# Sign counts on ScalarE, thirty of fifty rows on VectorE: a graph network kernel's first chunks

## What is computed

```python
h = relu(layernorm(x))
deg = segment_sum(ones, src)                   # edges of each node
feat = h * clip(deg, 1)**-0.5
x = x + relu(segment_sum(feat[src], dst)) @ W.T + b
h = relu(layernorm(x))
msg = h[src] @ W_msg.T + b_msg + edge_embed[edge_type]
x = x + gru_cell(segment_sum(msg, dst), h)     # gates r, z, n
```

## Time and profile before

| | us |
|---|---|
| median of 3 runs | 938.37 (937.33 to 938.54) |
| the profiled execution | 936.48 |
| its span in the profile | 934.5 |
| TensorE busy (share of the span) | 848.2 (91%) |
| VectorE busy | 776.1 (83%) |
| ScalarE busy | 503.8 (54%) |

### The profile page before, as it was taken

How to read it: one execution, slowest core, us unless ns; L and a number is a source line. 1 busy time by engine, 2 the same in 40 slices (tenths; PEclk the granted TensorE clock), 3 DMA queues, 4 the chain that set the end, 5 groups by cost and what they waited for, 6 DMA issues and landing times.

```text
span 934.5 us, 21030 instructions
## 1 busy us (share of the span) xinstructions
PE 848.2 (91%) x8962; PEld 757.1 (81%) x8962; DVE 776.1 (83%) x1043; ACT 503.8 (54%) x924; POOL 86.5 (9%) x77
## 2 busy tenths in 40 slices
PE   2264999999999999999999999799999999999996
PEld 2252888888888888888888888688898889888985
DVE  6897999999999999999999982386667667766876
ACT  1479588888888888888888873111111110111111
POOL 6880203010020010100000000000000000000000
PEclk9999999999999999999999999899999999999999
DMA  4541434356443365433355300766776676667650
GB/s 111 113 163 46 163 144 174 145 208 231 155 170 149 144 234 208 160 145 149 144 208 207 154 7 13 200 237 223 280 279 233 242 287 257 236 251 294 244 220 21
DMA packets 38595, 169.41 MB, mean 181 GB/s; under 512 B 8140, under 2 KB 21651, under 8 KB 35552
## 3 DMA queue, kind: packets, MB, share of 16 engines
q1 hardware_dynamic: 32188, 160.25, 45.7%
q0 software_dynamic: 6000, 6.48, 2.6%
q10 hardware_dynamic: 308, 1.28, 0.5%
HBM read 87.93 MB, written 80.00 MB: 180 GB/s over the span
## 4 chain that ended last, share of the span: by engine, by line
PE 74%; ACT 12%; POOL 4%; DVE 4%; issue 3%; DMA 2%; SPq 0%; ACTq 0%; DVEq 0%; POOLq 0%
PE ps L1285 27%; PE ps L1156 23%; PE ps L1145 12%; ACT ring L952 7%; POOL tab L483 3%; PE ps L1249 2%; PE ps L1250 2%; PE ps L1168 2%; PE ps L1182 2%; DMA tab<-dst 1%; ACT tab L963 1%; PE ps L1255 1%; PE ps L1254 1%; DVE work L725 1%; DMA tab<-dst,row_i 1%
## 5 line engine op out<-in xcount | busy, mean ns | idle before, releaser
L1145 PE MATMUL ps<-work 128*128 128x106 f16 x3125 | 429.0, 216 | 48.7 <-ACT ring L952 29.7
L1156 PE MATMUL ps<-ring,tab 125*128 125x250 f16 x2500 | 413.2, 272 | 0.7 <-ACT ring L957 0.7
L952 ACT ACTIVATE ring<-ps 128x848 f16<-128x848 f32 x375 | 329.8, 882 | 73.9 <-PE ps L1145 68.6
L1145 PEld LDWEIGHTS ps<-work 128*128 128x128 f16 x3125 | 288.5, 101 | 68.3 <-ACT ring L952 28.2
L1285 PE MATMUL ps<-ring,tab 125*128 125x250 f16 (+1 forms) x2500 | 276.8, 269 | 0.0
L1285 PEld LDWEIGHTS ps<-ring,tab 125*128 125x128 f16 (+1 forms) x2500 | 242.5, 97 | 28.6
L1156 PEld LDWEIGHTS ps<-ring,tab 125*128 125x128 f16 x2500 | 244.4, 98 | 25.1 <-ACT ring L957 0.9
L725 DVE TENSOR_TENSOR work<-iota_row,mch 128x3906 f16<-128x3906 f16 x100 | 222.0, 2220 | 5.6 <-PE ps L1145 4.5
L732 DVE TENSOR_TENSOR work<-iota_w,mch 128x1550 f16<-128x1550 f16 x200 | 188.3, 983 | 0.0
L813 DVE TENSOR_TENSOR work<-work,ring 125x3250 f16<-125x3250 f16 (+1 forms) x92 | 161.6, 1779 | 0.0
L1094 ACT ACTIVATE tab<-ps,bg 128x250 f32<-128x250 f32 x25 | 11.7, 470 | 155.4 <-PE ps L1250 155.4
(11 more groups left out here) (167 smaller groups left out, 595.1 us busy)
## 6 DMA issues: line engine op xcount, KB each, us to landing
adjacency<-ring SPq DMA_DIRECT2D x23, 2937.5 KB
ring<-adjacency SPq DMA_DIRECT2D x46, 812.5 KB, 6.4
ring<-adjacency SPq DMA_DIRECT2D x46, 750.0 KB, 9.2
adjacency<-ring SPq DMA_DIRECT2D x23, 183.1 KB
h_turned<-hst SPq DMA_DIRECT2D x25, 125.0 KB, 2.0
tab<-h_turned SPq DMA_DIRECT2D x25, 125.0 KB, 2.0
out<-x_sb SPq DMA_DIRECT2D x25, 125.0 KB
x_sb<-x SPq DMA_DIRECT2D x3, 560.0 KB
```

Of the source, the lines that this page charges most:

```text
L952: act.activation(to(x * 2 * u, 2, x), ps[:, s:s + 2, 0:x * SLOTS].rearrange("p b (x h) -> p h b x", h=SLOTS), ACT.Copy).then_inc(sem("evac ...
L1145: last = pe.matmul(ps[:, 2 * (u % 2) + i // BANKW, o:o + WCOLS], lohot[:, s, k, :], combo[:, s, k, :], start=True, stop=True)
L1156: mm = pe.matmul(psD[c % 2], tabv[0][P, h, s, :], adj[c % 2][P, h, :], start=i == 0, stop=i == 2 * BLOCKS - 1)
```

## The change

1. ScalarE counts the first nodes too, for steps 3 and 4: `search_odd` becomes `search_signs`, which is called with "odd" as before and with "even" for these steps, over 66 values with a new limit `thr_even`, right behind the odd counts. VectorE's `search_runs` for steps 3 and 4 go; in their place one `take_runs` behind chunk 1's first batch makes `run0` and `run_i` of both steps out of the sums.
2. `ON_ACT` is 2 instead of 3: VectorE makes batches 2, 3 and 4 of the rows, 30 of 50.
3. ScalarE's row keys for chunks 3 to 5 come after unit 6 of chunk 1 instead of after unit 10.
4. In chunk 0 VectorE takes the statistics of x's fourth fifth before it unpacks chunks 1 and 2, instead of after.
5. The factor: `a0 = (var + eps)` is made with the statistics, max and product are one instruction, and 4096 goes into the square root's scale.

```diff
-ON_ACT = 3
+ON_ACT = 2
...
+SIGNED = [("odd", g) for g in range(STEPS[3][1])] + [("even", g) for g in range(*STEPS[3])] + \
+         [("odd", g) for g in range(*STEPS[4])] + [("even", g) for g in range(*STEPS[4])] + \
+         [("odd", g) for g in range(*STEPS[5])]
...
+            gp.iota(thr_even[:, :], [[2 * WIN, CHUNKS]], base=-1, channel_multiplier=2 * BLOCKS,
+                    allow_small_or_imprecise_dtypes=True)
...
+        def take_runs(v, ch, first, last):
+            at = slice(STEPS[first][0], STEPS[last][1])
+            signed = SIGNED.index(("even", STEPS[last][1] - 1)) + 1
+            for k in range(JUNK):
+                v.wait_ge(sem(f"signs{k}"), len(range(k, signed, JUNK)))
+            ch.did(v.scalar_tensor_tensor(run0[P, at], even_sum[P, at], 0.5, row[P, at], ALU.mult, ALU.add))
+            ch.wait()
+            ch.did(v.tensor_scalar(run0[P, at], run0[P, at], HLEN / 2, None, ALU.add))
+            ch.wait()
+            v.tensor_scalar(run_i[P, at], run0[P, at], 3.0, None, ALU.mult).then_inc(sem("run_i"), last + 1 - first)
...
+            v.scalar_tensor_tensor(a0[P, :], deg[P, :], 1.0, a0[P, :], ALU.max, ALU.mult).then_inc(sem("a_square"), 1)
             ch.did(v.tensor_reduce(flags[P, 3:4], odd_sum[P, :], AX, ALU.max))
-            ch.wait()
-            ch.did(v.tensor_scalar(degm[P, :], deg[P, :], 1.0, None, ALU.max))
-            ch.did(v.tensor_scalar(a0[P, :], xvar[P, :], 1.0 / D, EPS, ALU.mult, ALU.add))
-            ch.wait()
-            v.tensor_tensor(a0[P, :], a0[P, :], degm[P, :], ALU.mult).then_inc(sem("a_square"), 1)
...
-            ch.wait()
-            ch.did(v.tensor_scalar(a0[P, :], a0[P, :], HSCALE, None, ALU.mult))
...
                         if b == 1:
+                            row_stats(v, ch, 3, 0, XB)
                             unpack(v, ch, 1, 2)
-                            row_stats(v, ch, 3, 0, XB)
-                            search_runs(v, ch, 3)
...
-                        if b == 3:
-                            search_runs(v, ch, 4)
                     if c == 1:
+                        if b == 0:
+                            take_runs(v, ch, 3, 4)
...
-        def search_odd(act, m):
+        def search_signs(act, which, m):
...
+            limit, n, to = {"odd": (thr_odd, CAND, odd_sum), "even": (thr_even, HLEN, even_sum)}[which]
...
-                    if c == 1 and u == ROOT_UNIT + ON_ACT_UNITS:
-                        high_rows(act, 3)
+                    if c == 1 and u == ROOT_UNIT + 2:
                         row_keys(act, AHEAD, AHEAD)
...
-                        search_odd(act, ODD_AT[u])
+                        search_signs(act, "odd", ODD_AT[u])
+                        if ODD_AT[u] < 5:
+                            search_signs(act, "even", ODD_AT[u])
```

More of the change, by code:

```diff
@@ L71 @@
 runs_in0 runs_in1 runs_in2 runs_in3 runs_in4 runs_in5
-squares sq_sum wm_norm gsc_set scaled g_col emb_in odd0 odd1 a_square a_root scale0 h0 rows_v tab0_hi tab0
+squares sq_sum wm_norm gsc_set scaled g_col emb_in signs0 signs1 a_square a_root scale0 h0 rows_v tab0_hi tab0
 fields lo_keys turned mch_keys mch onehot built spent evac adj_out0 adj_out1 types_moved
@@ L187, in gnn @@
         thr_odd = sb("thr_odd", [128, CHUNKS], F32)
+        thr_even = sb("thr_even", [128, CHUNKS], F32)
         thr_key = sb("thr_key", [128, CHUNKS], F32)
@@ L205, in gnn @@
         deg = sb("deg", [128, BLOCKS], F32)
-        degm = sb("degm", [128, BLOCKS], F32)
         outdeg = sb("outdeg", [128, BLOCKS], F32)
@@ L261, in gnn @@
         totals, at = carve(early, at, CHUNKS)
+        even_sum, at = carve(early, at, CHUNKS)
         tri, at = carve(early, at, 128)
@@ L645, in join_stats @@
             ch.wait()
+            ch.did(v.tensor_scalar(a0[P, :], xvar[P, :], 1.0 / D, EPS, ALU.mult, ALU.add))
+            ch.wait()
         def scale_weights(v, ch):
@@ L676, in scale_rows @@
             for k in range(JUNK):
-                v.wait_ge(sem(f"odd{k}"), len(range(k, CHUNKS, JUNK)))
+                v.wait_ge(sem(f"signs{k}"), len(range(k, len(SIGNED), JUNK)))
             ch.did(v.scalar_tensor_tensor(run1[P, :], odd_sum[P, :], 0.5, row[P, :], ALU.mult, ALU.add))
@@ L789, in vector_build @@
                         if b == 2:
-                            rows_vector(v, ch, 3)
-                            rows_vector(v, ch, 4)
+                            for t in range(ON_ACT, TBATCHES):
+                                rows_vector(v, ch, t)
                         if b >= 2:
@@ L897, in vector_layer1 @@
             post1_out_vector(v, last)
-        def search_odd(act, m):
+        def search_signs(act, which, m):
             a, b = STEPS[m]
+            limit, n, to = {"odd": (thr_odd, CAND, odd_sum), "even": (thr_even, HLEN, even_sum)}[which]
             act.wait_ge(sem(f"cand_in{m}"), 16 * (b - a))
             for g in range(a, b):
-                positive(act, sem(f"odd{g % JUNK}"), g // JUNK)
-                act.activation(signs[P, g % JUNK, :], cand[P, g, :], ACT.Sign, bias=thr_odd[P, g:g + 1], scale=-2.0,
-                               accum_out=odd_sum[P, g:g + 1]).then_inc(sem(f"odd{g % JUNK}"), 1)
+                made, k = divmod(SIGNED.index((which, g)), JUNK)
+                positive(act, sem(f"signs{k}"), made)
+                act.activation(signs[P, k, 0:n], cand[P, g, 0:n], ACT.Sign, bias=limit[P, g:g + 1], scale=-2.0,
+                               accum_out=to[P, g:g + 1]).then_inc(sem(f"signs{k}"), 1)
         def row_keys(act, g, n):
@@ L1032, in scalar_main @@
             act.activation(gsc[:, :], psB, ACT.Sqrt, bias=least[:, :]).then_inc(sem("wm_norm"), 1)
-            search_odd(act, 0)
-            search_odd(act, 1)
+            search_signs(act, "odd", 0)
+            search_signs(act, "odd", 1)
             row_keys(act, 0, 1)
             turn_scalar(act, 0)
-            search_odd(act, 2)
+            search_signs(act, "odd", 2)
             for c in range(CHUNKS):
@@ L1045, in scalar_main @@
                         act.wait_ge(sem("a_square"), 1)
-                        act.activation(a0[P, :], a0[P, :], ACT.Sqrt).then_inc(sem("a_root"), 1)
+                        act.activation(a0[P, :], a0[P, :], ACT.Sqrt, scale=1.0 / HSCALE ** 2).then_inc(sem("a_root"), 1)
                         act.wait_ge(sem("scale0"), 1)
```

5 lines of the change are left out of this document (3 added, 2 removed).

## The result

The changed kernel takes **940.53 us** (median of 6 executions, 939.43 to 941.93), the kernel before 938.12 in the same comparison (936.38 to 938.87). The ratio is 1.0031 with a 95% interval of 1.0019 to 1.0042, so +2.9 us (+1.8 to +3.9). That is outside what I called "within 0.2%" (1.9 us), and the median lies 0.4 us above my range. Its profiled execution took 939.75 us with a span of 937.8. Of before that was 936.48 and 934.5 us.

A forecast was written before the change was run, and what follows sets the result against it. The chain to TensorE's bank at 119.42 us was taken as the bound: GpSimd's gathers, ScalarE, then VectorE. +3.26 − 0.22 + 2.58 − 4.93 = +0.69 us at VectorE's pnm gave 939.1 us, range 935.9 to 940.1.

The forecast's parts named there:

- within 0.2%: Whole kernel's time: a difference of up to 1.9 us either way, which measurement cannot tell from no change; chance 0.76.
- my range: Measured time of the changed kernel: 935.9 to 940.1 us, including 0.6 us for the spread of the runs.
- The rule of held issues: GpSimd's gather issues: one that begins inside a VectorE one-hot is held and ends 1.08 us after that instruction.
- GpSimd's extra iota costs between nothing and 0.17 … I take nothing: GpSimd ahead of the first gather: the added iota was counted as free, covered by VectorE's and TensorE's own work.
- The landing lag of 2.19 us: Last candidate gather: from the end of its issue on GpSimd to ready data takes 2.19 us, as before.
- The even counts: ScalarE's counts for steps 3 and 4: 0.34 us each, between 0.28 and 0.40, with VectorE waiting 3 us.
- The short factor, the rows and the row keys: VectorE up to pnm: −0.22 us for one operation less, +2.58 for ten more rows, −4.93 for the removed wait.
- TensorE has room: TensorE up to 119.42 us: 80 products start at 96.1, its bank comes 0.86 us before release, not setting the end.
- the slot: Rival: GpSimd's issue at 39.31 gets in ahead of the one-hot; −1.2 us, 937.2 us, chance 0.25.
- GpSimd is not delayed: Rival: the candidate gather issues come no later than before; −2.3 us, 936.1 us, chance 0.16.
- slow products: Rival: TensorE's 80 products of chunk 0 stay at the low clock level; +6 us, 944.5 us, chance 0.05.
- Carrying the profile's difference to the median: Whole kernel: the profiled execution's 1.89 us below the median was added, turning a span of 935.2 into 939.1 us.

The follow-up runs named there:

- run 4: Changed kernel with two statistics of x's fourth fifth made twice, right ahead of chunk 0's one-hots of batch 2: 938.32 us against 937.43 before.
- run 5: Changed kernel with the statistics of x's fourth fifth moved back behind the unpacking of chunks 1 and 2: 939.66 us against 937.59 before.
- run 2: Changed kernel with the iota of thr_even moved late, behind the one of thr_key: 939.22 us against 937.59 before.
- run 1: Kernel before with one more iota of 25 elements on GpSimd behind the one of thr_odd: 938.50 us against 937.59 before.
- run 3: Changed kernel with SyncE's write of chunk 0's adjacency held until step 5's gathers are in: 939.21 us against 937.43 before.
- run 7: Changed kernel with 20 rows on VectorE again and the row keys back at their old place: 943.05 us against 938.39 before.
- run 6: Kernel before with 30 rows on VectorE and ScalarE's row keys four units sooner: 935.29 us against 937.59 before.
- run 12: Kernel before with 30 rows on VectorE, row keys sooner, TensorE's constants wait behind 25 matmuls and the short factor: 934.12 us against 938.39 before.
- run 8: Kernel before with only the row keys of chunks 3 to 5 four units sooner: 937.55 us against 938.39 before.

## Why the prediction was wrong, step by step

- **The rule of held issues** (in the part on GpSimd's issues): right, and shown by run 4. In the fourteen profiles, between 24 and 66 us, 167 issues began inside a one-hot, and 166 ended 1.06 to 1.10 us after it. Its two held issues of the changed order took 3.2 and 3.1 us as replayed, each at the predicted time + 0.8 to 0.9. Incomplete: run 5's issue is the one left, and lost four times in a row.
- **"GpSimd's extra iota costs between nothing and 0.17 … I take nothing"**: this step failed. It cost 0.91 in the changed kernel's start; undoing it gave back 0.8 (run 2), and alone it cost 0.86 there and +0.8 in the median (run 1). The cover I named (VectorE's and TensorE's own work) was not there: TensorE's first matmuls wait for GpSimd's last constant, and between the iota and that stood two operations that run into VectorE's instruction. Of the kernels with the early iota (the changed one, runs 1, 3, 4, 5, 7) all six profiles show 0.8 and 1.0 us; of the eight others two do (runs 6 and 12). So 0.9 is the difference of these two profiles; against a median of executions that collide now and then the price is somewhat less. I had written down the rule for gather issues and did not ask where else it applies.
- **The landing lag of 2.19 us**: carried over from an order in which SyncE's write was issued 0.91 us after the gather's issue had ended. The gather's end moved by 4.35 us and the write by 3.33, so they met. Mis-sized by 0.71; shown by run 3 and by the lags by distance.
- **The even counts** (0.34 at pitch): the trace has 0.33. `take_runs` waits 2.93, I said 3. The last one-hot starts at 60.19; predicted 59.1 and 0.91 for the start are 60.0. This is the 0.2 that is left.
- **The short factor, the rows and the row keys**: −2.57 predicted, −2.54 measured. Rows and keys alone are −2.35 by the terms and −2.3 in the kernel before (run 6). But they are no two separate terms: the keys alone give −0.9 and not −4.9 (run 8).
- **TensorE has room**: right in what it says of the end, not of the way there. The 80 products start at 98.83 and not at 96.1, and take 8.75 us instead of 9.63. Its bank is at 121.93, where it waits 1.48 us for ScalarE, which waited 1.55 for `pnm`.
- **The rivals**: the slot was not won (the one-hot at 40.07 is ahead of 40.12), though 0.05 us decided; with 0.4 us of extra work it is won. "GpSimd is not delayed" and "slow products" did not come: over 96 to 106 us the granted clock was 1.00 in the changed kernel and 0.91 in the one before.
- **Carrying the profile's difference to the median**: I took 1.89 us. The changed kernel's profiled execution is only 0.78 under its median. Before's had the shortest exchange between the layers of all (last section), and it lacked the collision at the start, as six of the eight without the early iota do. How much of its 1.89 either makes is not measured. From `pnm`'s +2.52 and before's median the time would have been 940.6.
- **The range** ended 0.4 us too low. It held ±0.36 for one small count and 0.6 for the spread of the runs, and nothing for the two terms that I had carried over as constants.

## What to carry to other kernels

In this kernel gather issues that began inside a two-input VectorE instruction were held, and `ident` and `nident` took longer there (0.78 and 1.04 us for 0.52 and 0.53). Not everything was: the iota and the memset behind them take 0.13 and 0.20 us inside that instruction in both kernels, and issues that began inside VectorE's statistics (one input) took 1.21, as at 45.42. So an added or moved instruction is to be priced at the next such meeting behind it, not at its own length: 0.1 us made the first gather 0.9 late, and 0.4 us of extra work won 2. A DMA's landing time is no constant: when a chain moves, look at which large transfers do not move by the same amount. An edit that removes a wait is worth what the next wait leaves of it, on the same engine or on another, so find that one and pay for both together (−0.9 alone, −2.3 as a pair).

## What the runs showed of the hardware that I had not expected

**A held issue can miss the gap.** In 166 cases of 167 it ended 1.06 to 1.10 us after the end of the one-hot in which it had begun; in run 5 one ended only after the fourth, and what was different there is open.

**The time from `pnm` to the end varies by itself.** In thirteen of the fourteen profiles the stretch from `pnm` to the start of TensorE's last 30 products of the first layer is 457.5 to 457.7 us, so a shift at 119 us does arrive unchanged where VectorE sets the end. In run 8, where TensorE does, it is 458.8. Then comes the exchange between the layers, whose last transfers take 13 to 16 us. Chains of waits, kernel before and then run 1:

```profile
575.48 3.22 PE ps L1156 x30
...
588.36 13.00 DMA tab<-dst
601.38 1.89 DVE tab L669
```

```profile
577.00 3.22 PE ps L1158 x30
...
588.56 16.18 DMA tab<-dst
604.76 1.89 DVE tab L671
```

From the 30 products to VectorE's first instruction of the second layer it is 25.90 us in the kernel before and 27.76 in run 1; over the fourteen profiles it goes from 25.90 to 28.01, with no order by kernel. A single span so says nothing to better than 2 us, while `pnm` says it to 0.1, as long as VectorE sets the end.
